# Own step tables for the first batches, and row fills at other places, in a fused macaron block (feed-forward, attention, feed-forward)

## The reference

```python
x = x + 0.5 * ffn(layernorm(x))
x = x + attention(layernorm(x))      # 16 heads of 8, rotary, softmax over 512 keys
x = x + 0.5 * ffn(layernorm(x))      # same weights as the first
```

## Time and profile before

| | |
|---|---|
| runs | 550.89, 562.03, 566.96 us, median 562.03 |
| the profiled execution | 559.28 us, span 557.5 us |
| TensorE busy, mean granted clock | 473.2 us (85%), 0.938 |
| VectorE, ScalarE, POOL busy | 438.8 us, 389.1 us, 229.7 us |
| stretch 0 to 77 us: TensorE, VectorE, ScalarE, POOL | 33.55, 51.93, 36.09, 19.39 us |
| stretch 77 to 139 us (62 us) | 59.80, 54.11, 48.76, 31.09 us |
| row fills on ScalarE | 6 of 3.60 us |

### The profile page before, as it was taken

One profiled execution on the slowest core, in us unless ns is written; L12 is line 12 of the kernel. 1 busy time (PEld: TensorE's weight loads), 2 busy tenths in 40 slices (PEclk: granted clock), 3 DMA queues, 4 the chain that ended last, 5 costly groups with the idle time before them and its releaser, 6 DMA issues.

```text
span 557.5 us, 10137 instructions
## 1 busy us (share of the span) xinstructions
PE 473.2 (85%) x2628; PEld 165.2 (30%) x2628; DVE 438.8 (79%) x1020; ACT 389.1 (70%) x754; POOL 229.7 (41%) x350
## 2 busy tenths in 40 slices
PE   2141889999999989999899889999999999998851
PEld 1121232333233333433233223333233323322211
DVE  6646999887998797978897688978897789888025
ACT  5556149787878776688768676878768787777840
POOL 8100156326662555437552564436553534112310
PEclk9985599999999997999899998999899999999995
DMA  6013411221122212221123112221222022200000
GB/s 170 7 47 89 127 51 48 88 86 50 49 87 86 69 50 63 71 88 30 55 84 106 41 48 86 76 68 30 71 79 89 31 76 87 76 3 2 20 1 19
DMA packets 27967, 34.89 MB, mean 63 GB/s; under 512 B 6278, under 2 KB 21260, under 8 KB 27916
## 3 DMA queue, kind: packets, MB, share of 16 engines
q1 hardware_dynamic: 26284, 33.94, 20.1%
q10 hardware_dynamic: 1632, 0.39, 0.3%
HBM read 21.34 MB, written 8.39 MB: 53 GB/s over the span
## 4 chain that ended last, share of the span: by engine, by line
PE 60%; DVE 18%; issue 8%; ACT 7%; POOL 5%; DVEq 1%; DMA 0%; POOLq 0%; ACTq 0%; SPq 0%
PE ot L1120 19%; PE sc L1107 16%; PE st L1096 13%; DVE negmax L893 8%; PE misc L1085 3%; PE misc L1043 3%; ACT probs L645 2%; PE misc L1060 2%; ACT feat_k L535 2%; DVE stats_f L761 1%; DVE amax_f L785 1%; PE misc L1068 1%; PE misc L1038 1%; PE misc L1077 1%; PE misc L1051 1%
## 5 line engine op out<-in xcount | busy, mean ns | idle before, releaser
L893 DVE TENSOR_REDUCE negmax<-sc 128x1 f32<-128x512 f32 x512 | 331.5, 683 | 60.8 <-PE sc L1107 60.0
L645 ACT ACTIVATE probs<-st 128x512 f32<-128x512 f32 x512 | 272.3, 602 | 78.4 <-PE st L1096 75.4
L1107 PE MATMUL sc<-feat_k,feat_q 96*128 96x512 bf16 x512 | 189.4, 398 | 11.8 <-DVE negmax L893 11.1
L1096 PE MATMUL st<-feat_q,feat_k 99*128 99x512 bf16 x512 | 160.3, 386 | 7.8 <-ACT probs L645 6.8
L1120 PE MATMUL ot<-probs,vfeat 128*32 128x512 f32 x1024 | 139.5, 618 | 1.0 <-ACT probs L645 1.0
L1107 PEld LDWEIGHTS sc<-feat_k,feat_q 96*128 96x128 bf16 x512 | 50.1, 98 | 167.8 <-DVE negmax L893 126.2
L1096 PEld LDWEIGHTS st<-feat_q,feat_k 99*128 99x128 bf16 x512 | 49.9, 99 | 80.7 <-ACT probs L645 51.9
L452 POOL TENSOR_SCALAR maxparts<-negmax 128x16 bf16<-128x16 f32 x32 | 8.3, 258 | 70.3 <-DVE negmax L893 70.3
L1027 PE MATMUL misc<-identb,xq_f 128*128 128x128 bf16 x64 | 6.8, 235 | 34.9 <-DVE xq_f L837 34.8
L494 POOL TENSOR_TENSOR xres<-xres,onorm 128x128 f32 (+1 forms) x31 | 14.1, 454 | 53.3 <-DVE onorm L910 53.3
L636 ACT COPY outT<-ot 128x512 f32<-128x512 f32 x32 | 18.8, 586 | 18.7 <-PE ot L1120 18.7
(11 more groups left out here) (134 smaller groups left out, 488.1 us busy)
## 6 DMA issues: line engine op xcount, KB each, us to landing
feat_q<-parts_q SPq DMA_DIRECT2D x96, 96.0 KB
feat_k<-parts_k SPq DMA_DIRECT2D x96, 96.0 KB
qkswap<-qkpre SPq DMA_DIRECT2D x32, 128.0 KB, 2.0
parts_q<-qkparts_q SPq DMA_DIRECT2D x24, 128.0 KB, 2.4
parts_k<-qkparts_k SPq DMA_DIRECT2D x24, 128.0 KB, 2.3
xres<-in_L_attn_x_dram SPq DMA_DIRECT2D x8, 256.0 KB, 4.6
out_dram<-xres SPq DMA_DIRECT2D x8, 256.0 KB, 2.4
feat_q<-maxrows ACTq DMA_DIRECT2D x32, 12.0 KB
```

What stands on the lines that cost most here:

```text
L645: nc.scalar.activation(probs[:, s % US, j * S:(j + 1) * S], st[:, bank(2 * s + j), :], ACT.Exp, scale=SCALE).then_inc(exp_done, 1)
L893: nc.vector.tensor_reduce(negmax[:, g, j:j + 1], sc[:, bank(16 * g + j), :], AX.X, ALU.max, negate=True).then_inc(sc_maxed, 1)
L1096: nc.tensor.matmul(st[:, bank(2 * s + j), :], feat["k"][par][0:MROWS, h, kb * P:(kb + 1) * P], feat["q"][par][0:MROWS, h, :], start=True, ...
L1107: nc.tensor.matmul(sc[:, bank(16 * g + j), :], feat["q"][par][0:SROWS, h, t * P:(t + 1) * P], feat["k"][par][0:SROWS, h, :], start=True, s ...
```

## The change

The steps in a table hold for all batches. The change adds FIRST, with tables of its own for batch 0's projection and for batch 1's first feed-forward and projection, and a helper `turns` that every `slot` function asks in place of `turns_of_batch`. Batch 1's feed-forward moves from slot -1 into slot -2 and the start of slot -1; it is taken out of `hurried`, so its norm goes to ScalarE and scaling and quant go to POOL. Batch 1's projection moves from steps 20 to 40 to steps 11 to 33 of slot -1 (its loads keep their steps); batch 0's rotation and splitting are drawn together, with the keys' first product ahead of the queries' swapped one. The semaphore of the rotation is divided in one for queries and one for keys, which this order needs.

Of the six row fills, that of zeros in `feat_k1` and in `feat_q1` go ahead of ScalarE's set-up, and that of ones in `feat_k1` stands behind the copy `xnT` of batch 0, where `feat_q1`'s stood. The other three keep their places. The counts that others wait for follow.

```diff
+FIRST = {
+    ("pj", 0): dict(PROJ, qk=(27, 27), swap=(27, 28), rope=(28, 29, 28, 30), high=(29, 30), rest=(30, 30), mid=(31, 31),
+                    low=(31, 31), v=30, write=33, load=(34, 35)),
+    ("f1", 1): dict(FFN1, stats=-17, rstd=-15, norm=-12, amax=-6, scale=-3, expo=1, quant=1, turn=5, mul=6),
+    ("pj", 1): dict(PROJ, stats=11, rstd=12, norm=13, turn=19, qk=(20, 22), swap=(21, 23), rope=(21, 23, 26, 27), high=(25, 29),
+                    rest=(28, 30), mid=(29, 31), low=(30, 32), v=24, write=33),
+}
...
-            return known(b) and (n, b) in (("f1", 0), ("pj", 0), ("f1", 1), ("f2", B - 1))
+            return known(b) and (n, b) in (("f1", 0), ("pj", 0), ("f2", B - 1))
...
+        def turns(b, par, s, n, key, first, i=None, later=0):
+
+            table = dict(f1=FFN1, f2=FFN2, pj=PROJ)[n]
+            step = (table[key] if i is None else table[key][i]) + later
+            out = [(nb, npar) for nb, npar in turns_of_batch(b, par, s, step, first) if not known(nb) or (n, nb) not in FIRST]
+            for (name, nb), own in FIRST.items():
+                if known(b) and name == n:
+                    step = (own[key] if i is None else own[key][i]) + later
+                    out += [turn for turn in turns_of_batch(b, par, s, step, first) if turn[0] == nb]
+            return out
...
                     if known(b) and b < 2:
-                        sp.wait_ge(init_act, ACT_STEPS - 3 + 3 * b)
+                        sp.wait_ge(init_act, ACT_STEPS - 1 + b)
...
             nc.scalar.activation(fscale[:, NB:NB + 1], invf[:, :], ACT.Exp, scale=RANGE * LN2).then_inc(init_act, 1)
+
+            feature_rows("k", 1, 0)
+            feature_rows("q", 1, 0)
...
-                    if known(b) and b == -1 and s == PROJ["mid"][1] % STEPS + 1:
-                        feature_rows("k", 1, 0)
-                        feature_rows("k", 1, 1)
...
                         copy_xnT(nb)
                         if known(nb) and nb == 0:
-                            feature_rows("q", 1, 0)
+                            feature_rows("k", 1, 1)
...
-            pe.wait_ge(init_act, 7)
+            pe.wait_ge(init_act, 9)
...
-            pe.wait_ge(init_act, 10)
+            pe.wait_ge(init_act, 12)
```

More of the change, by code:

```diff
@@ L520, in slot @@
                     for i in range(2):
-                        for nb, _ in turns_of_batch(b, par, s, PROJ["rest"][i], 2):
+                        for nb, _ in turns(b, par, s, "pj", "rest", 2, i=i):
                             if not hurried("pj", nb):
                                 rest(nb, i)
-                        for nb, _ in turns_of_batch(b, par, s, PROJ["low"][i], 2):
+                        for nb, _ in turns(b, par, s, "pj", "low", 2, i=i):
                             if not hurried("pj", nb):
@@ L606, in high @@
             def high(b, i):
[L608 removed]
+                act.wait_ge(rope_step[i], 3 * b + 3)
                 if after(96 * b):
@@ L658, in slot @@
                         copy_out(nb, g)
-                    for n, at, first in (("f2", FFN2, -1), ("f1", FFN1, 2), ("pj", PROJ, 2)):
+                    for n, first in (("f2", -1), ("f1", 2), ("pj", 2)):
                         for half in range(2):
-                            for nb, _ in turns_of_batch(b, par, s, at["norm"] + half, first):
+                            for nb, _ in turns(b, par, s, n, "norm", first, later=half):
                                 if not hurried(n, nb):
@@ L927, in slot @@
                         invert_sums(nb, g)
-                    for n, at, first in (("f2", FFN2, -1), ("f1", FFN1, 2)):
-                        for nb, _ in turns_of_batch(b, par, s, at["mul"] + 1, first):
+                    for n, first in (("f2", -1), ("f1", 2)):
+                        for nb, _ in turns(b, par, s, n, "mul", first, later=1):
                             add_ffn(n, nb)
@@ L936, in slot @@
                             attended(nb, g)
-                    for n, at, first in (("f2", FFN2, -1), ("f1", FFN1, 2), ("pj", PROJ, 2)):
-                        for nb, _ in turns_of_batch(b, par, s, at["stats"], first):
+                    for n, first in (("f2", -1), ("f1", 2), ("pj", 2)):
+                        for nb, _ in turns(b, par, s, n, "stats", first):
                             stats(n, nb)
-                        for nb, _ in turns_of_batch(b, par, s, at["stats"] + 1, first):
+                        for nb, _ in turns(b, par, s, n, "stats", first, later=1):
                             aggregate(n, nb)
@@ L954, in slot @@
                         for later in (1, 2):
-                            for nb, _ in turns_of_batch(b, par, s, at["amax"] + later, first):
+                            for nb, _ in turns(b, par, s, n, "amax", first, later=later):
                                 if not hurried(n, nb):
                                     block_scales(n, nb, 2 * later)
-                        for nb, _ in turns_of_batch(b, par, s, at["scale"], first):
+                        for nb, _ in turns(b, par, s, n, "scale", first):
                             if hurried(n, nb):
                                 scale(n, nb)
-                        for nb, _ in turns_of_batch(b, par, s, at["expo"], first):
+                        for nb, _ in turns(b, par, s, n, "expo", first):
                             exponents(n, nb, 0)
@@ L965, in slot @@
                                 exponents(n, nb, 2)
-                        for nb, _ in turns_of_batch(b, par, s, at["expo"] + 1, first):
+                        for nb, _ in turns(b, par, s, n, "expo", first, later=1):
                             if not hurried(n, nb):
                                 exponents(n, nb, 2)
-                        for nb, _ in turns_of_batch(b, par, s, at["quant"], first):
+                        for nb, _ in turns(b, par, s, n, "quant", first):
                             if hurried(n, nb):
```

83 lines of the change are left out of this document (41 added, 42 removed).

## The result

| | before | after | predicted |
|---|---|---|---|
| median, 20 executions each | 562.42 us | 564.75 us | 558.6 (551 to 566) |
| ratio of the executions compared | | 1.0151, 95% [1.0108, 1.0194] | 0.996 (-2.1 of 560.7 us) |
| profiled execution, its span | 559.28, 557.5 | 561.60, 559.6 | 557.2 |

The time lies inside the range and "within 2%" came true, but the sign is wrong. The ratio leaves out executions more than 1.5% above a kernel's fastest, which here drops more of the kernel before's; that is why it is further from 1 than the medians, which differ by 0.4%. Two more timed sets gave 1.0065 [1.0024, 1.0107] and 1.0042 [0.9999, 1.0086].

What follows compares the result with a forecast made beforehand. Two chains of waits were taken to set slot 0's start, with VectorE's maxima the bound after 57.00. The terms -3.2 -1.2 +2.8 +0.7 -1.2 gave -2.1 us from 560.7, so 558.6, range 551 to 566.

Steps and rivals of the forecast that it cites:

- The fills, the splitting, batch 1's feed-forward (-3.2): Start before slot 0: both paths to the first maximum shrink, so it comes at 53.8 instead of 57.00, -3.2 us.
- the set-up: ScalarE's start: after the two moved fills it would end near 18.4, at no cost, with 0.9 to 1.1 us cover.
- The pauses under the maxima (+2.8): VectorE's first maxima: batch 1's projection on TensorE makes pauses of 4.0 us in all, +2.8 us.
- The held exponentials (+0.7): ScalarE's queue: copies waiting on POOL hold the first exponential until 77.2, so VectorE waits for the 34th score, +0.7 us.
- Slot 0 relieved (-1.2): Slot 0: value product, five ScalarE copies and eight POOL operations leave it, -1.2 us, bounds 0 and -2.3.
- the second rival: TensorE's clock stays low, rising only at 82: +1.9 us, 562.6; dead if 1.00 at the 13th score; chance 0.15.
- the sign of being wrong that I had named: Changed profile: the forecast is wrong if TensorE's clock is 0.50 beyond 70.
- the low clock over the scores of the kernel before: TensorE's scores before the change: their low clock was said to agree with the skill's rule that small idles lower it.
- The sum: Whole kernel: all terms together give -2.1 us, 558.6 from 560.7.
- the third rival: Start: set-up cover fails or batch 1's quantization comes 2 later, pauses eat the gain; no net effect, 560.7; chance 0.2.
- Nothing behind slot 0 changes: Later slots: each is bound from within, so slots 1 to 7 keep their lengths and the difference stays.

Runs made afterwards that it cites:

- e10: Of the change only the moved fills and the table of batch 1's feed-forward, both projections on their old steps; ratio to the kernel before 1.0065.
- e11: Of the change the moved fills, the last in step 0 of slot -1, and batch 0's projection table; batch 1's feed-forward hurried in its old place; ratio 1.0015.
- e5: Changed kernel with the queries' swapped product moved from step 23 to 25 and the keys' rest, middle and low parts to steps 34 to 38; ratio to before 0.9954.
- e8: Changed kernel with the queries' swapped product and sum on POOL moved from step 23 to 25, their high copy from 25 to 27; ratio to before 1.0054.
- the first four experiments: Changed kernel plus idle products (1.0063), without batch 1's projection table (0.9937), with only the moved fills (1.0056), with batch 1's last splitting steps later (1.0003); ratios to before.
- e7: e5 plus three extra products of 512 columns per step in steps 24 to 31 of slot -1; ratio to before 0.9954.

## Why the prediction was wrong

**The fills, the splitting, batch 1's feed-forward (-3.2): right, a little more.** Every step lies within 0.5 us of its number, but the addition, 50.51 for 51.0, and the aggregation behind it made the first maximum 52.95 rather than 53.8: -4.05. e10 and e11 show that both paths had to shrink. Two readings were off without weight: the set-up, which by 13.31 + 4.9 would end at 18.2 and not 18.4, ended at 18.15, with a cover of 1.35 us; and the page's row has its low digits in slices 0 to 3 alone, slice 4 reads 8.

**The pauses under the maxima (+2.8): right in kind.** 3.05 us in place of 4.0, at 57.84, 60.65 and 66.06; the clock had risen by 62 as said. The last of the 15 maxima from 66.06 ends at 75.11 and is the 31st, so the 30th ends near 74.5: 3.2 us ahead of before, where I had worked out 1.6.

**The held exponentials (+0.7): right in place, wrong in weight.** They were held until 76.05 (77.2 forecast) by exactly the operations named. What I priced was VectorE's wait; what it cost, by e5, was 1.8 to 2.3 us at the first reciprocal, and 3.3 in e8, whose chain ends 2 us later. In two of five traces the chain was later still by 1.7 to 2.2 us.

**Slot 0 relieved (-1.2): the step that failed.** From the first exponential to the first reciprocal it takes 22.79 us, before 21.90: a loss of 0.89, and over the five traces 0.3 on average (21.8 to 22.8), where 1.2 was to be gained. I had checked whether the clock rises in time and declared the second rival dead once it stood at 1.00 at the 13th score. It did stand there, and fell ten microseconds later; the sign of being wrong that I had named, the clock at 0.50 beyond 70, was there in all five traces (from 71.2 to 72.4 on in three, behind the sparse scores; from 69 on in the two with the late swap, behind the stop at the turned maxima). The change takes the keys' projection and the value product out of the stretch that carried the clock; what is left is one score of 0.39 us per maximum of 0.605, 3.94 of 6 us. With the stretch filled (e7) the same piece takes 20.06 us, so the relief itself was 1.8, more than I took, and the fall took 2.2 to 2.7 us, more than the whole of it (2.2 by the pair of traces with equal first exponentials). The second rival named the clock, but had it fail to rise instead of falling, and that its +1.9 is near the +2.3 of the medians is luck, since the start was not later at all. The Trainium skill's rule that was cited there (TensorE: Matmul & The Clock Gate, section "A second HAM failure mode: psum-queue depth-cycling"), of the clock falling back while small idles recur, points at this fall: idles of 0.2 us recur from 69 to 73. But the kernel before has idles of 0.2 to 0.35 us between 73 and 80 and kept 1.00 there, so the rule alone does not say which stretch loses the clock. Nor was the low clock over the scores of the kernel before an agreement with it: the clock had stood at 0.50 since 38 us and did not fall back there.

**The sum.** -2.1 was forecast; at the first reciprocal five traces of after and four of before show -0.15. By its outcome at the start the case is the third rival's, no net effect, but by none of its causes: the maxima did start 4 us earlier. The two terms that lost the lead are the held exponentials, priced too low, and slot 0, where a gain was counted and the clock was not.

**Nothing behind slot 0 changes: narrowed, not settled.** The traces show slots of equal length at an equal clock, and no kernel's falls to be more frequent. But the medians of the three timed sets were 2.3, 1.9 and 4.1 us above before, and executions under 560 us were 22 of 78 for the kernel before and 2 of 44 for the changed one. The start explains none of that. Outside the profiled span an execution takes 1.8 us before and 2.0 after, which is 0.2 of it. The rest goes with the clock: in the second and the last set the mean granted clock of a timed execution was 0.9335 for the kernel before (57 executions) and 0.927 for the changed one (24), and a straight line of span against clock through each kernel's executions gives, at 0.93, 562.0 and 561.7 us. So in these two sets no cost of the split semaphores of the rotation, or of any step that takes longer at a given clock, is to be seen. (In the set of the first four experiments the moved fills alone lay 3.0 us above the kernel before at nearly the same clock, 0.940 against 0.941, which no trace explains.) Part of the lower mean belongs to the fall at 72: between 38 and 100 us the traces have 34.1 to 35.7 us at 0.50 before and 36.6 to 41.0 after, some 4 us more, which by an estimate from these numbers is 0.0036 of the 0.0065. Why the rest falls more often in the timed executions, by chance or by the shift of the start, was not tried and stays open.

The version that beats both kernels is the change without its table for the second batch's projection, best with the last fill in step 0 of the slot before the first: 0.9948 [0.9901, 0.9996] and 0.9997 [0.9955, 1.0038], mean 5.4 and 2.1 us below before. That is under 1% and only the first of its two sets excludes no change.

## What to carry to other kernels

Where a change moves work off TensorE's queue, look at what stays there: the moved projection had been what kept its clock up, and without it the stretch lost at half speed what it had gained. Before work is put ahead of the first instruction of the next stage, add up the chain on the other engine that it waits for, and price the delay for the stage and not only for the engine that you take for the bound. And in a kernel whose times form groups some us apart, read the start of the difference from traces at a landmark, and count the groups before believing a ratio of 1%.

## What the hardware showed beside that

The queries' four swap transfers, issued at 61.0 right behind 24 feature loads, landed in three traces of the changed kernel so that GpSimd could start at 63.72 to 63.74, and in two at 65.46 and 65.91. The same instructions in the same order, some 2 us apart; why, the traces do not show:

```profile
63.72 1.26 POOL L490 TENSOR_TENSOR qkswap<-qkswap,ropeT 128x512 f32<-128x512 f32 x1 [1.42 <-DMA qkswap<-qkpre]
```

```profile
65.46 1.26 POOL L490 TENSOR_TENSOR qkswap<-qkswap,ropeT 128x512 f32<-128x512 f32 x1 [3.13 <-DMA qkswap<-qkpre]
```

The first is of after, the second of its second trace. In the kernel before, where the swap is issued at 73.37, 7 us behind the last load, four traces of the first exponential lie within 0.14 us.
